# Left-over 64 channels of the projections as half-height matmul pairs, in units of two groups

## The chip, the cores and the metric

The kernel runs on one core of one Trainium2 chip. The metric is the device time of one execution in microseconds (us). A core has TensorE (PE in the profile; its weight loads are PEld), VectorE (DVE), ScalarE (ACT), GpSimd (POOL) and SyncE (SP, here only an issuer of DMAs), 16 DMA engines, the on-chip SBUF of 128 partitions and PSUM of 8 banks with 512 fp32 per partition.

## The reference

x has R = 128 rows, C = 192 columns and E = 192 channels. It is group-normalised, then goes through an attention with 12 heads of D = 16 channels in which two columns attend to each other, summed over all rows (row weights `sw` come from a softmax of their own). All in fp32.

```python
Q = (x @ Wq).reshape(B, R, C, H, D) * scaling * sw
K = (x @ Wk).reshape(B, R, C, H, D)
V = (x @ Wv).reshape(B, R, C, H, D)
QK = jnp.einsum('brihd,brjhd->bhij', Q, K)
...
attn = jax.nn.softmax(QK, axis=-1)
out = jnp.einsum('bhij,brjhd->brihd', attn, V)
...
x = x + _L0_conv_ref(_gn(x), ...)
```

## The kernel before

**Precision.** Each fp32 operand of a matmul is split into an fp16 high part and an fp16 low part, and a product is the sum of high x high, high x low and low x high.

**Prologue.** x is loaded, its statistics are taken on DVE (`statistics`, L600), and it is transposed chunk by chunk (a chunk is CI = 8 columns) by PE (`x_transposes`, L872), normalised on DVE and ACT, and split in high and low (ACT L492, DVE L694, POOL L442). SyncE stores the transposed chunks in pairs to a DRAM scratch `xt_dram` with seven transfers per pair (L333 to L339). In between PE computes the scores of the row weights (L927, L933). These are transposed back in three parts by `weights_back` (L962 to L964, the matmuls are at L949), and ACT copies each part to SW (L516, semaphore `s_sw`).

**Layout of the transposed x.** 192 channels are 128 + 64. A loaded chunk in XT[b] has three regions of 8 x 128 columns: the highs of the 128 channels, their lows, and a third region for the other 64 channels, whose upper and lower 64 partitions are, before, the highs and the lows of the same column. Eight columns stand as four even ones and four odd ones. The weights of the 64 channels stand twice in WP, in partitions 0 to 63 and 64 to 127.

**Projections.** There are two head halves, h = 0 and h = 1 (h0 and h1 below). `project(h, t, steps)` (L970) makes Q and K of six heads and V of all twelve for h0 (384 outputs per column, CW[0]), and Q and K of the other six heads for h1 (192, CW[1]). A group is SI[h] = 2 or 4 columns and fills two PSUM banks; four groups have buffers (`projected`, L243). A column takes five matmuls with the transposed x stationary and the weights moving:

```python
mm(po, xh0, WP[:, 0, 0, wc], start=True, stop=False)
mm(po, xh0, WP[:, 1, 0, wc], start=False, stop=False)
mm(po, xl0, WP[:, 0, 0, wc], start=False, stop=False)
mm(po, x1, WP[:, 0, 1, wc], start=False, stop=False)
ins = mm(po, x1, WP[:, 1, 1, wc], start=False, stop=True)
```

h0 has 96 groups, h1 48, unrolled by 8 in a hardware loop. For each group ACT copies the highs of V (L532, h0 only) and of K (L535); DVE multiplies Q by the row weights (L767), and subtracts for the lows of V (L773, h0 only) and K (L776, which frees the PSUM buffer, `s_kvl`); ACT copies the highs of Q (L521) and POOL subtracts for its lows (L451). PE waits ahead of group n for `s_kvl` of group n - 4 (L977), at a new chunk for its load (L976), and in the first turn of h0 for parts of the row weights (L981 to L984), whose banks it reuses; in the first turn of h1 for the last reads of the attention before it.

**SyncE in h0.** Chunks are loaded into two buffers (`load_xt`, L343). V goes to DRAM from two buffers, two transfers per chunk up to column 127 (L355), four with rows of 192 bytes from column 128 on (L359, `store_v`); ACT waits for the store of two chunks before (L531). In h1 there are four load buffers; the third and fourth lie where the attention of h0 had its last output tiles, so their first loads wait for output stores (L404).

**Attention.** Per head 16 x 5 matmuls (L1053 to L1057) and four fp32 transposes (L1038 to L1041) with softmax on DVE and ACT; then attention times V (L1024), the residual on DVE (L839) and stores issued by ACT (L569, L572).

## Time and profile before

| | us |
|---|---|
| median of 3 runs | 647.25 (646.57 to 648.66) |
| the profiled execution | 645.96 |
| its span in the trace | 644.2 |
| PE busy | 518.9 (81%), 4984 matmuls |
| DVE busy | 435.5 (68%) |
| ACT busy | 251.3 (39%) |
| POOL busy | 225.7 (35%) |
| HBM traffic | 95.60 MB read, 56.62 MB written |

The shares are averages over stages with different limits, so they are read by stage. "Busy" of PE is modelled from pipelined matmuls: one matmul's duration is longer than the distance to the next one's start, and what a matmul costs in a stream is that distance. The granted clock is a fraction of the higher of TensorE's two levels. A wait is shown as idle time with what ended it.

### The profile page before, as it was taken

The page shows a single profiled execution, that of the slowest core. Times are in us where ns is not written, and L with a number is a line of the kernel's source. Part 1 is how long each engine was busy: PE and PEld are TensorE (multiplying, and loading weights), DVE is VectorE, ACT ScalarE, POOL GpSimd, SP SyncE. Part 2 cuts the span into 40 slices and gives each one's busy share as a digit, 9 for nine tenths or more (in the row PEclk, how much of TensorE's full clock was granted, in tenths as well). Part 3 has the DMA queues.
Part 4 walks back from the last instruction along what each step waited for, and adds up shares of the span by engine and source line. Part 5 has one row for each costly group of instructions (what it writes and reads, how often), then busy time and mean ns, then how long its engine had stood idle before and what let it go on. Part 6 is the DMA issues. An engine that isn't in the chain of part 4 may idle for free.

```text
span 644.2 us, 14355 instructions
## 1 busy us (share of the span) xinstructions
PE 518.9 (81%) x4984; PEld 426.1 (66%) x4984; DVE 435.5 (68%) x981; ACT 251.3 (39%) x555; POOL 225.7 (35%) x231
## 2 busy tenths in 40 slices
PE   0040298998539999999998999969499997999884
PEld 0030177998416666666665998849499997998773
DVE  3899847799915666666665566936277774566954
ACT  0030236688306555555554111323255552112242
POOL 1010024688303333333333000638255663000674
PEclk9996557899559999999998999979799998999988
DMA  8993004798965888888998999999877766899998
GB/s 279 404 424 142 0 1 141 197 244 243 249 207 157 236 249 240 242 246 237 237 243 150 276 288 295 309 338 272 261 235 243 242 196 147 263 268 304 285 269 231
DMA packets 207258, 152.82 MB, mean 237 GB/s; under 512 B 170032, under 2 KB 190064, under 8 KB 206448
## 3 DMA queue, kind: packets, MB, share of 16 engines
q1 hardware_dynamic: 155296, 132.14, 70.5%
q10 hardware_dynamic: 51920, 20.11, 12.5%
q8 instruction: 28, 0.46, 0.3%
q14 instruction: 14, 0.11, 0.0%
HBM read 95.60 MB, written 56.62 MB: 236 GB/s over the span
## 4 chain that ended last, share of the span: by engine, by line
PE 64%; DVE 12%; SPq 7%; DMA 5%; ACTq 4%; issue 3%; POOL 3%; ACT 1%; POOLq 0%; DVEq 0%
PE PS L993 7%; PE PS L994 7%; PE PS L995 7%; PE PS L996 7%; PE PS L997 7%; DVE EXTRA L600 6%; PE PS L1024 6%; PE PS L872 3%; PE PS L1053 3%; DVE BIG L839 3%; PE PS L1054 3%; PE PS L1055 3%; PE PS L1056 3%; PE PS L1057 3%; PE PS L911 2%
## 5 line engine op out<-in xcount | busy, mean ns | idle before, releaser
L451 POOL TENSOR_TENSOR BIG<-EXTRA,BIG 128x192 f32 (+1 forms) x144 | 106.5, 740 | 165.8 <-ACT BIG L521 165.6
L767 DVE TENSOR_TENSOR EXTRA<-PS,SW 128x192 f32<-128x192 f32 (+1 forms) x144 | 73.2, 508 | 96.0 <-ACT BIG L535 95.7
L993 PE MATMUL PS<-WP,EXTRA 128*128 128x384 f16 (+1 forms) x384 | 111.0, 289 | 21.4 <-DMA EXTRA<-xt_scratch 21.4
L994 PE MATMUL PS<-WP,EXTRA 128*128 128x384 f16 (+1 forms) x384 | 111.1, 289 | 0.0
L995 PE MATMUL PS<-WP,EXTRA 128*128 128x384 f16 (+1 forms) x384 | 111.0, 289 | 0.0
L996 PE MATMUL PS<-WP,EXTRA 128*128 128x384 f16 (+1 forms) x384 | 110.8, 289 | 0.0
L997 PE MATMUL PS<-WP,EXTRA 128*128 128x384 f16 (+1 forms) x384 | 110.8, 288 | 0.0
L1024 PE MATMUL PS<-BIG,EXTRA 128*128 128x256 f16 x768 | 88.9, 279 | 10.2 <-ACT EXTRA L578 10.0
L459 POOL TENSOR_TENSOR BIG<-BIG,EXTRA 64x512 f32<-64x512 f32 x36 | 45.1, 1265 | 135.0 <-DVE BIG L839 108.9
L1024 PEld LDWEIGHTS PS<-BIG,EXTRA 128*128 128x128 f16 x768 | 75.8, 100 | 22.5 <-issue 10.2
L442 POOL TENSOR_TENSOR BIG<-EXTRA,BIG 128x1024 f16<-128x1024 f32 x24 | 53.4, 2227 | 71.2 <-ACT BIG L492 70.9
L535 ACT CAST BIG<-PS 128x192 f32 (+3 forms) x144 | 55.1, 383 | 43.8 <-PE PS L997 43.8
L532 ACT CAST EXTRA<-PS 128x384 f16<-128x384 f32 x96 | 46.0, 479 | 62.0 <-PE PS L997 50.5
L521 ACT CAST BIG<-EXTRA 128x192 f32 (+3 forms) x144 | 60.5, 420 | 2.0 <-DVE EXTRA L767 2.0
L839 DVE SCALAR_TENSOR_TENSOR BIG<-PS,small,BIG 128x512 f32<-128x512 f32 x72 | 49.0, 737 | 17.6 <-PE PS L1024 17.4
L993 PEld LDWEIGHTS PS<-WP,EXTRA 128*128 128x128 f16 x384 | 37.9, 99 | 34.3 <-issue 13.1
L776 DVE TENSOR_TENSOR BIG<-PS,BIG 128x192 f32 (+3 forms) x144 | 59.9, 416 | 0.0
L600 DVE BATCH_NORM_STATS2 EXTRA<-BIG 128x6 f32<-128x192 f32 x192 | 50.3, 335 | 13.4 <-DMA BIG<-in_x 13.3
L578 ACT ACTIVATE EXTRA<-PS,small 64x512 f32<-64x512 f32 x48 | 30.6, 681 | 60.9 <-PE PS L1024 27.2
L1053 PE MATMUL PS<-BIG 128*128 128x192 f16 x192 | 48.4, 252 | 5.9 <-POOL BIG L451 5.9
L773 DVE TENSOR_TENSOR EXTRA<-PS,EXTRA 128x384 f16<-128x384 f32 x96 | 52.6, 548 | 0.0
L872 PE MATMUL PS<-ident,BIG 128*128 128x128 f32 x288 | 45.0, 321 | 5.9 <-DVE EXTRA L637 4.2
(155 smaller groups left out, 931.2 us busy)
## 6 DMA issues: line engine op xcount, KB each, us to landing
EXTRA<-xt_scratch SPq DMA_DIRECT2D x48, 512.0 KB, 3.6
BIG<-in_x SPq DMA_DIRECT2D x6, 3072.0 KB, 21.6
EXTRA<-xt_scratch SPq DMA_DIRECT2D x48, 256.0 KB, 3.8
v_scratch<-EXTRA SPq DMA_DIRECT2D x32, 384.0 KB, 4.2
BIG<-v_scratch SPq DMA_DIRECT2D x16, 768.0 KB, 6.9
BIG<-in_x SPq DMA_DIRECT2D x12, 768.0 KB, 9.3
out_x<-BIG ACTq DMA_DIRECT2D x12, 768.0 KB, 6.8
xt_scratch<-BIG SPq DMA_DIRECT2D x12, 512.0 KB, 3.3
```

The source lines that it names most:

```text
L451: pool.tensor_tensor(QA[:, :, bass.ds(SI[h] * n + low, SI[h])], TQ[h][g % 4], QA[:, :, bass.ds(SI[h] * n, SI[h])], ALU.subtract).then_inc( ...
L600: ins = v.bn_stats(ST[:, g, c, :], xv[:, :, g * GC:(g + 1) * GC])
L767: v.tensor_tensor(TQ[h][g % 4].rearrange("p (m d) i -> p m d i", d=D), ps[:, :, 0:EH].rearrange("p i (m d) -> p m d i", d=D), swv.unsqueez ...
L839: v.scalar_tensor_tensor(o, PS[0:rows, attended_bank(m), :].rearrange("p (r e) -> p r e", r=RI), mxb[0:rows, WV:WV + 1], o, ALU.mult, ALU. ...
L872: ins = nc.tensor.transpose(PS[:, 3 * (c % 2) + k, q * P:(q + 1) * P], X[:, at:at + P], ident[:, :])
L993: mm(po, xh0, WP[:, 0, 0, wc], start=True, stop=False)
L994: mm(po, xh0, WP[:, 1, 0, wc], start=False, stop=False)
L995: mm(po, xl0, WP[:, 0, 0, wc], start=False, stop=False)
L996: mm(po, x1, WP[:, 0, 1, wc], start=False, stop=False)
L997: ins = mm(po, x1, WP[:, 1, 1, wc], start=False, stop=True)
L1024: ins = mm(po[:, :, a, :], stationary, moving, start=j == 0, stop=j == len(terms) - 1)
L1053: mm(p0, QA[:, m, 0:P], kh, start=first, stop=False)
```

## The change

1. `project` works on units of two groups (`for u in range(SPT[h] // 2)`): first all waits of both groups, then two parts, each for both groups. `full_rows` has the three matmuls per column on the 128 channels. `half_rows` has the 64 left-over channels: for two neighbouring columns three steps (high x high, high x low, low x high), in each of which one matmul uses partitions 0 to 63 for the even column and one partitions 64 to 127 for the odd one. The low x low product is gone. In every other unit the half part comes first.
2. The third region of XT therefore has the even column's highs and lows in partitions 0 to 63 and the odd column's in 64 to 127; the stores to DRAM go from seven to five per pair of chunks.
3. The two columns of a step lie in different PSUM banks. For h0 they did already; for h1 `projected` now lets neighbouring columns alternate between the two banks. The reads of ACT and DVE follow that: the product with the row weights is two instructions per group in h1, the copy and the subtraction of K have one more dimension.

```diff
--- before.py
+++ after.py
@@ -153,7 +153,7 @@
 
         s_x = [sem(f"x_loaded{c}") for c in range(NXC)]
         s_params = sem("params_loaded")
-        STORES = 16 * 7
+        STORES = 16 * 5
         V_STORED = 32 * 8 + 64 * 4
         s_wld = sem("weights_loaded")
         N_WEIGHTS = 5 * 3
@@ -244,7 +244,7 @@
 
             b = 2 * ((g + 3) % 4)
             ps = PS[:, b:b + 2, :]
-            return ps if h == 0 else ps.rearrange("p a (b n) -> p (a b) n", b=2)
+            return ps if h == 0 else ps.rearrange("p a (b n) -> p b a n", b=2)
 
 
 
@@ -326,17 +326,15 @@
                 sp.wait_ge(s_ld, c + 2)
                 stored = s_sp[min(c, 1)]
                 full = xt_dram[c // 2, :, 0:4 * CI * R].rearrange("p (c a n) -> p c a n", a=2, n=512)
-                rest = xt_dram[c // 2, :, 4 * CI * R:6 * CI * R].rearrange("p (c a n) -> p c a n", a=2, n=512)
+                rest = xt_dram[c // 2, :, 4 * CI * R:6 * CI * R].rearrange("p (c n) -> p c n", n=512)
                 src = BIG[:, c * CI * E:(c + 2) * CI * E].bitcast(fp16)
                 src = src.rearrange("p (c t n) -> p c t n", t=3, n=512)
                 even, mixed, odd = (src[:, :, t, :] for t in range(3))
                 sp.dma_start(full[:, :, 0, :], even).then_inc(stored, 16)
                 sp.dma_start(full[0:E1, :, 1, :], mixed[E1:P]).then_inc(stored, 16)
                 sp.dma_start(full[E1:P, :, 1, :], odd[0:E1]).then_inc(stored, 16)
-                for s in range(2):
-                    to = rest[s * E1:(s + 1) * E1]
-                    sp.dma_start(to[:, :, 0, :], mixed[0:E1, s::2, :]).then_inc(stored, 16)
-                    sp.dma_start(to[:, :, 1, :], odd[E1:P, s::2, :]).then_inc(stored, 16)
+                sp.dma_start(rest[0:E1], mixed[0:E1]).then_inc(stored, 16)
+                sp.dma_start(rest[E1:P], odd[E1:P]).then_inc(stored, 16)
             sp.wait_ge(s_sc, NCH // 2)
             sp.wait_ge(s_sp[0], STORES)
 
@@ -532,8 +530,13 @@
                             nc.scalar.copy(VS[b][:, at:at + SI[h], :, 0, :],
                                            ps[:, :, 2 * EH:2 * EH + E].rearrange("p i (h e) -> p i h e", h=2)
                                            ).then_inc(s_kvh[h], 1)
-                        nc.scalar.copy(KA[:, :, bass.ds(SI[h] * n, SI[h])],
-                                       ps[:, :, EH:2 * EH].rearrange("p i m -> p m i")).then_inc(s_kvh[h], 1)
+                        if h == 0:
+                            nc.scalar.copy(KA[:, :, bass.ds(SI[h] * n, SI[h])],
+                                           ps[:, :, EH:2 * EH].rearrange("p i m -> p m i")).then_inc(s_kvh[h], 1)
+                        else:
+                            nc.scalar.copy(KA[:, :, bass.ds(SI[h] * n, SI[h])].rearrange("p m (b a) -> p m b a", a=2),
+                                           ps[:, :, :, EH:2 * EH].rearrange("p b a m -> p m b a")
+                                           ).then_inc(s_kvh[h], 1)
                         if g or not isinstance(t, int):
                             q_high(n - 1, g - 1)
 
@@ -764,18 +767,25 @@
                         when(dve, s_ql[h], n - 3)
                         swv = SW[:, bass.ds(si * n * H, si * H)].rearrange("p (i m) -> p m i", m=H)
                         swv = swv[:, h * HALF:(h + 1) * HALF, :]
-                        v.tensor_tensor(TQ[h][g % 4].rearrange("p (m d) i -> p m d i", d=D),
-                                        ps[:, :, 0:EH].rearrange("p i (m d) -> p m d i", d=D),
-                                        swv.unsqueeze(2).to_broadcast([P, HALF, D, si]),
-                                        ALU.mult).then_inc(s_tq[h], 1)
+                        tq = TQ[h][g % 4].rearrange("p (m d) i -> p m d i", d=D)
+                        for i in range(0, si, 2):
+                            pq = ps[:, :, 0:EH] if h == 0 else ps[:, i // 2, :, 0:EH]
+                            ins = v.tensor_tensor(tq[:, :, :, i:i + 2], pq.rearrange("p i (m d) -> p m d i", d=D),
+                                                  swv[:, :, i:i + 2].unsqueeze(2).to_broadcast([P, HALF, D, 2]),
+                                                  ALU.mult)
+                        ins.then_inc(s_tq[h], 1)
                         if h == 0:
                             vs = VS[b][:, at:at + si, :, :, :]
                             v.tensor_tensor(vs[:, :, :, 1, :],
                                             ps[:, :, 2 * EH:2 * EH + E].rearrange("p i (h e) -> p i h e", h=2),
                                             vs[:, :, :, 0, :], ALU.subtract)
-                        v.tensor_tensor(KA[:, :, bass.ds(si * n + C, si)],
-                                        ps[:, :, EH:2 * EH].rearrange("p i m -> p m i"),
-                                        KA[:, :, bass.ds(si * n, si)], ALU.subtract).then_inc(s_kvl[h], 1)
+                        kl, kh = (KA[:, :, bass.ds(si * n + o, si)] for o in (C, 0))
+                        if h == 0:
+                            pk = ps[:, :, EH:2 * EH].rearrange("p i m -> p m i")
+                        else:
+                            pk = ps[:, :, :, EH:2 * EH].rearrange("p b a m -> p m b a")
+                            kl, kh = (q.rearrange("p m (b a) -> p m b a", a=2) for q in (kl, kh))
+                        v.tensor_tensor(kl, pk, kh, ALU.subtract).then_inc(s_kvl[h], 1)
 
                 if h:
                     dve.wait_ge(s_lo[0], NB)
@@ -967,35 +977,52 @@
 
             pe.wait_ge(s_wl, len(W_PARTS))
 
-            def project(h, t, steps):
+            def project(h, t):
                 wc = slice(h * CW[0], h * CW[0] + CW[h])
-                for g in steps:
-                    n = SPT[h] * t + g
-                    b, at = divmod(g * SI[h], CI)
-                    if at == 0:
-                        pe.wait_ge(s_xt[h][b], 32 * (t + 1))
-                    when(pe, s_kvl[h], n - 3)
-                    if h and isinstance(t, int) and g < 4:
-                        pe.wait_ge(s_ad[0], 2 * NB - 6 + 2 * g)
-                        pe.wait_ge(s_ol[0], NB - 3 + g)
-                    if h == 0 and isinstance(t, int) and g in range(1, PARTS + 1):
-                        if g < PARTS:
-                            weights_back(g)
-                        pe.wait_ge(s_sw, g)
-                    ps = projected(h, g)
+
+                def full_rows(ps, b, at, opens):
                     for i in range(SI[h]):
-                        il = at + i
-                        po = ps[:, i, 0:CW[h]]
-                        slot = (il % 2) * (CI // 2) + il // 2
+                        po = ps[:, i, 0:CW[h]] if h == 0 else ps[:, i // 2, i % 2, 0:CW[h]]
+                        slot = ((at + i) % 2) * (CI // 2) + (at + i) // 2
                         xh0 = XT[b][:, slot * R:(slot + 1) * R]
                         xl0 = XT[b][:, (CI + slot) * R:(CI + slot + 1) * R]
-                        x1 = XT[b][:, (2 * CI + slot) * R:(2 * CI + slot + 1) * R]
-                        mm(po, xh0, WP[:, 0, 0, wc], start=True, stop=False)
-                        mm(po, xh0, WP[:, 1, 0, wc], start=False, stop=False)
-                        mm(po, xl0, WP[:, 0, 0, wc], start=False, stop=False)
-                        mm(po, x1, WP[:, 0, 1, wc], start=False, stop=False)
-                        ins = mm(po, x1, WP[:, 1, 1, wc], start=False, stop=True)
-                    ins.then_inc(s_pj[h], 1)
+                        for j, (xs0, w) in enumerate(((xh0, 0), (xh0, 1), (xl0, 0))):
+                            ins = mm(po, xs0, WP[:, w, 0, wc], start=opens and i < 2 and j == 0,
+                                     stop=not opens and j == 2, skip_group_check=True)
+                    return ins
+
+                def half_rows(ps, b, at, opens):
+                    for even in range(0, SI[h], 2):
+                        for j, (s, w) in enumerate(((0, 0), (0, 1), (1, 0))):
+                            for i, rows in ((0, slice(0, E1)), (1, slice(E1, P))):
+                                po = ps[:, i, 0:CW[h]] if h == 0 else ps[:, even // 2, i, 0:CW[h]]
+                                o = (2 * CI + s * (CI // 2) + (at + even) // 2) * R
+                                ins = mm(po, XT[b][rows, o:o + R], WP[rows, w, 1, wc],
+                                         start=opens and even == 0 and j == 0, stop=not opens and j == 2,
+                                         skip_group_check=True)
+                    return ins
+
+                for u in range(SPT[h] // 2):
+                    for g in (2 * u, 2 * u + 1):
+                        n = SPT[h] * t + g
+                        b, at = divmod(g * SI[h], CI)
+                        if at == 0:
+                            pe.wait_ge(s_xt[h][b], 32 * (t + 1))
+                        when(pe, s_kvl[h], n - 3)
+                        if h and isinstance(t, int) and g < 4:
+                            pe.wait_ge(s_ad[0], 2 * NB - 6 + 2 * g)
+                            pe.wait_ge(s_ol[0], NB - 3 + g)
+                        if h == 0 and isinstance(t, int) and g in range(1, PARTS + 1):
+                            if g < PARTS:
+                                weights_back(g)
+                            pe.wait_ge(s_sw, g)
+                    parts = (full_rows, half_rows) if u % 2 == 0 else (half_rows, full_rows)
+                    for j, part in enumerate(parts):
+                        for g in (2 * u, 2 * u + 1):
+                            b, at = divmod(g * SI[h], CI)
+                            ins = part(projected(h, g), b, at, j == 0)
+                            if j:
+                                ins.then_inc(s_pj[h], 1)
 
             def attended(h, m):
                 (n, hp), t = BLOCK[m // 2], m % 2
@@ -1026,9 +1053,9 @@
 
             for h in range(2):
 
-                project(h, 0, range(SPT[h]))
+                project(h, 0)
                 with pe.Fori(1, TURNS[h]) as t:
-                    project(h, t, range(SPT[h]))
+                    project(h, t)
 
                 def transposes(k):
                     lg = LG[k % 2]
```

Lines of the changed kernel are numbered anew: L990 is the matmul of `full_rows`, L1000 that of `half_rows`, L959 the transposes of `weights_back`, L773 and L788 DVE's product and subtraction of K.

PE in the body of h0's loop. Before, one group (two columns) of eight:

```order
L237 REGISTER_ALU
L993 MATMUL PS<-WP,EXTRA 128x384
L994 MATMUL PS<-WP,EXTRA 128x384
L995 MATMUL PS<-WP,EXTRA 128x384
L996 MATMUL PS<-WP,EXTRA 128x384
L997 MATMUL PS<-WP,EXTRA 128x384
L993 MATMUL PS<-WP,EXTRA 128x384
L994 MATMUL PS<-WP,EXTRA 128x384
L995 MATMUL PS<-WP,EXTRA 128x384
L996 MATMUL PS<-WP,EXTRA 128x384
L997 MATMUL PS<-WP,EXTRA 128x384
```

Now, all eight groups, in four units:

```order
L990 MATMUL PS<-WP,EXTRA 128x384 x12
L1000 MATMUL PS<-WP,EXTRA 128x384 x12
L237 REGISTER_ALU
L1000 MATMUL PS<-WP,EXTRA 128x384 x12
L990 MATMUL PS<-WP,EXTRA 128x384 x12
L237 REGISTER_ALU x2
L990 MATMUL PS<-WP,EXTRA 128x384 x12
L1000 MATMUL PS<-WP,EXTRA 128x384 x12
L237 REGISTER_ALU x2
L1000 MATMUL PS<-WP,EXTRA 128x384 x12
L990 MATMUL PS<-WP,EXTRA 128x384 x12
```

Ten matmuls per group have become twelve, six of them half-height (L1000), and these stand in runs of 24 but for the seams of the loop.

PE at the start of h0, with what it waits for. Before:

```order
L949 MATMUL PS<-ident,EXTRA 128x128 [waits row_weights_normalised]
L949 MATMUL PS<-ident,EXTRA 128x128 x5
L993 MATMUL PS<-WP,EXTRA 128x384 [waits row_weights_ready]
```

Now:

```order
L990 MATMUL PS<-WP,EXTRA 128x384 [waits row_weights_ready]
L990 MATMUL PS<-WP,EXTRA 128x384 x11
L1000 MATMUL PS<-WP,EXTRA 128x384 x12
L959 MATMUL PS<-ident,EXTRA 128x128 [waits row_weights_normalised]
L959 MATMUL PS<-ident,EXTRA 128x128 x5
L1000 MATMUL PS<-WP,EXTRA 128x384 [waits row_weights_ready]
```

The wait behind the last transposes is now for all three parts of the row weights, the one just issued included, where before it was for two, and the third was waited for a group later.

SyncE's list for one pair of chunks in the prologue. Before:

```order
L333 DMA xt_scratch<-BIG 128x4x512
L334 DMA xt_scratch<-BIG 64x4x512
L335 DMA xt_scratch<-BIG 64x4x512
L338 DMA xt_scratch<-BIG 64x2x512
L339 DMA xt_scratch<-BIG 64x2x512
L338 DMA xt_scratch<-BIG 64x2x512
L339 DMA xt_scratch<-BIG 64x2x512
```

Now:

```order
L333 DMA xt_scratch<-BIG 128x4x512
L334 DMA xt_scratch<-BIG 64x4x512
L335 DMA xt_scratch<-BIG 64x4x512
L336 DMA xt_scratch<-BIG 64x4x512
L337 DMA xt_scratch<-BIG 64x4x512
```

Four transfers of 64 x 2 runs have become two of 64 x 4.

## Rows read from the trace of the kernel before

**Rows 1.** Busy time by stage: us, then engines, granted clock, DMA share, GB/s.

```profile
188.00:349.50 161.50, 160.00 (x972) 96.32 (x971) 103.05 (x287) 92.74 (x290) 57.32 (x95) 0.98 0.87 221
...
463.00:538.00 75.00, 74.23 (x880) 73.83 (x880) 55.12 (x86) 38.59 (x87) 43.12 (x43) 0.98 0.66 217
```

**Rows 2.** Timeline of PE in h0: start us, us, instruction.

```profile
250.34 0.33 PE L993 MATMUL PS<-WP,EXTRA 128*128 128x384 f16 x1
...
251.96 0.33 PE L993 MATMUL PS<-WP,EXTRA 128*128 128x384 f16 x1
```

**Rows 3.** Timeline of PE and its weight loads (PEld) in h1.

```profile
489.94 0.25 PE L993 MATMUL PS<-WP,EXTRA 128*128 128x192 f16 x1
...
490.03 0.10 PEld L995 LDWEIGHTS PS<-WP,EXTRA 128*128 128x128 f16 x1
...
491.60 0.25 PE L993 MATMUL PS<-WP,EXTRA 128*128 128x192 f16 x1
```

**Rows 4.** Timeline of DVE catching up at the start of h0.

```profile
197.80 0.35 DVE L767 TENSOR_TENSOR EXTRA<-PS,SW 128x192 f32<-128x192 f32 x1
...
198.80 0.35 DVE L767 TENSOR_TENSOR EXTRA<-PS,SW 128x192 f32<-128x192 f32 x1
```

**Rows 5.** Timeline of PE, first projection matmul.

```profile
187.91 0.48 PE L993 MATMUL PS<-WP,EXTRA 128*128 128x384 f16 x1 [12.59 <-DMA EXTRA<-xt_scratch]
```

**Rows 6.** Waits at h1's loads: who for whom, us, times, longest.

```profile
PE PS L993 <- DMA EXTRA<-xt_scratch: 8.8, 1, 8.8
```

**Rows 7.** Timeline of PE and PEld, one round of attention transposes.

```profile
365.26 0.27 PE L1038 MATMUL PS<-ident,EXTRA 128*128 128x128 f32 x1
...
365.46 0.14 PEld L1039 LDWEIGHTS PS<-ident,EXTRA 64*128 64x128 f32 x1
...
365.46 0.27 PE L1039 MATMUL PS<-ident,EXTRA 64*128 64x64 f32 x1
...
366.12 0.10 PEld L1053 LDWEIGHTS PS<-BIG 128*128 128x128 f16 x1
366.13 0.26 PE L1053 MATMUL PS<-BIG 128*128 128x192 f16 x1
```

**Rows 8.** Timeline at the third part of the row weights.

```profile
194.43 0.82 PE L949 MATMUL PS<-ident,EXTRA 128*128 128x128 f32 x6
...
195.29 0.80 ACT L516 COPY SW<-PS 128x768 f32<-128x768 f32 x1 [1.91 <-PE PS L949]
```

**Rows 9.** Timeline of SyncE's queue, ACT and DVE in the last third of h0.

```profile
324.17 3.83 SPq L359 DMA_DIRECT2D v_scratch<-EXTRA  x4
...
331.67 0.48 ACT L532 CAST EXTRA<-PS 128x384 f16<-128x384 f32 x1 [2.17 <-DMA v_scratch<-EXTRA]
...
333.26 0.36 DVE L776 TENSOR_TENSOR BIG<-PS,BIG 128x192 f32 x1
```

**Rows 10.** Groups of h1 by line and shape: busy us, mean ns, idle before.

```profile
L451 POOL TENSOR_TENSOR BIG<-EXTRA,BIG 128x384 f32 x45 | 45.2, 1005 | 34.8 <-ACT BIG L521 34.8
...
L767 DVE TENSOR_TENSOR EXTRA<-PS,SW 128x384 f32<-128x384 f32 x44 | 35.8, 814 | 22.5 <-ACT BIG L535 22.5
L776 DVE TENSOR_TENSOR BIG<-PS,BIG 128x384 f32 x40 | 22.0, 550 | 0.0
```

**Rows 11.** Timeline of SyncE's queue, the last stores and the first load.

```profile
176.89 0.55 SPq L333 DMA_DIRECT2D xt_scratch<-BIG  x1
...
182.18 0.61 SPq L339 DMA_DIRECT2D xt_scratch<-BIG  x1
182.89 0.54 SPq L347 DMA_DIRECT2D EXTRA<-xt_scratch  x1
```

**Rows 12.** Busy time by single us in the store stage, columns as Rows 1.

```profile
171.00:172.00 1.00, 0.42 (x2) 0.45 (x3) 1.00 (x3) 0.84 (x1) 0.00 (x0) 0.50 0.59 144
...
179.00:180.00 1.00, 0.00 (x0) 0.00 (x0) 0.97 (x2) 0.00 (x0) 0.00 (x0) 0.50 1.00 291
180.00:181.00 1.00, 0.00 (x0) 0.00 (x0) 0.14 (x1) 0.00 (x0) 0.00 (x0) 0.50 0.95 207
```

## The prediction

> **What bounds the kernel now.** I read the busy times by stage first [rows 1]. In the two projection stages, from 188.0 to 349.5 us (first head half, in short h0) and from 463 to 538 us (second half, h1), the matmul row of TensorE (PE) is busy 160.0 of 161.5 us and 74.2 of 75.0; every other engine sits well below. Then the timeline of PE: in h0 the same line returns after one group of ten matmuls in 1.62 us [rows 2], so a matmul of 384 columns costs 0.162 us; in h1 it returns after twenty in 1.66 us [rows 3], so one of 192 columns costs 0.083 us. [...] So whatever shortens PE's list there shortens the run, until the next thing binds. I looked for that in three places: VectorE (DVE), which can serve h0 groups at a start-to-start of 1.00 us against PE's 1.62 [rows 4] (ScalarE, ACT, is busy 92.7 us of the stage [rows 1]); the stores of V in the last third of h0; and the head of the stage, where PE stands still 12.59 us until the first transposed x arrives [rows 5].
>
> **Fewer slots.** Call one full matmul time a slot. Before, a column takes 5 slots. Now it takes 3 full-height ones, and two columns share 3 steps in each of which one half-height matmul runs in rows 0 to 63 and another in rows 64 to 127. If the two of a step run at once, a column takes 4.5. h0: 96 groups of two columns, 10 slots become 9, 96 x 0.162 = **15.6 us less**. h1: 48 groups of four, 20 become 18, 0.166 each. The first four groups of h1 run before PE's wait of 8.8 us for a load [rows 6], so their gain is swallowed: 44 x 0.166 = **7.3 less**.
>
> **Does a pair really take one slot?** No row of before shows matmuls of two row groups alternating, so this is bounded. Best: nothing extra. Worst: one after the other, two slots a step; there are 3 x 96 steps in either half, 288 x (0.162 + 0.083) = 70.6 us. [...]
>
> **Switches of array shape.** Every unit of two groups goes once between full and half height (the reversed order in every other unit keeps the seams without one): 48 in h0, 24 in h1, 2 of them before the swallowed wait, so 70. The nearest rows are the four transposes of the attention stage, alternately 128 and 64 rows high [rows 7]. From the first one's start to the next full matmul's is 366.13 - 365.26 = 0.87 us with four changes. The same transposes with no change take 0.82 / 6 = 0.137 each [rows 8], and if the two small ones take half, 0.41 for all. The rest, 0.46, is 0.115 per change. They are fp32, whose weight load takes 0.14 against 0.10 [rows 7], so I take 0.08: 70 x 0.08 = **5.6 more**; ends 0 and 8.
>
> **Start of h0.** Two groups are now opened together, so all their waits stand ahead of both. The transposes of the third part of the row weights are issued ahead of group 2, and the wait for ACT's copy of them (group 3's) is right behind. Before, group 2's 1.6 us covered it. The copy starts 0.04 us after the transposes and takes 0.80 [rows 8], so with the signals PE waits about 1.0: **1.0 more** (0.8 to 1.2).
>
> **Rhythm of pairs.** Four buffers in PSUM are now two double ones: a unit waits for both groups of the unit before last. In h0 the second group of a unit is ready at T, the first 0.49 us earlier; ACT and DVE drain a group in 333.26 + 0.36 - 331.67 = 1.95 us when they start fresh [rows 9] and the second follows 1.0 behind [rows 4], about T + 2.5; it is due at T + 18 x 0.162 = T + 2.9. No wait, 0.4 us of slack. In h1 DVE's product took 0.81 [rows 10] and is now two of the form that takes 0.36 in h0 [rows 4]: 0.72, no loss. The subtraction (0.55 [rows 10]) now reads banks in another order; if it took 0.81 too, 0.72 + 0.81 = 1.53 against 1.50 per group would just bind, 1 to 2 us; I take 0. At the end of h1 the last two groups finish 0.5 us apart instead of 1.66, while GpSimd (POOL) takes 1.0 for each [rows 10]: attention waits **0.5 more**.
>
> **V stores.** From column 128 on V leaves in rows of 192 bytes. The four issues of a chunk take 3.83 us from 324.17 and ACT waits for their landing until 331.67 [rows 9], 7.5 us; PE does not feel it today because it is up to three groups ahead. ACT needs the V buffer two chunks later. With period P per chunk of 8 columns, the buffer is back at (last drained group) + 0.2 + 7.0 to 7.5, and PE stalls when that is later than the end of the next-but-one chunk's first unit: 1.5 P = 2.3 + 0.2 + 7.25, P = 6.5 us. That is today's period. So the 6 chunks for which this holds gain nothing of the net 0.4 each (6.5 less 36 slots of 0.162, two switches and the pairs' fixed part): **2.4 more** (0 to 4, as the transfers vary).
>
> **Stores of the transposed x.** Per chunk pair 7 transfers become 5; bytes and run lengths stay. At the end of the prologue SyncE issues back to back, 6.0 us per pair [rows 11], and the first projection waits behind that. Is it the issuing or the transfer? The DMA engines are 0.95 to 1.00 busy in the middle of a pair but 0.59 around its last two issues [rows 12], where 128 KB go out per 0.65 us. Larger issues close this hole: at full share 6.0 becomes about 5.6, times 10 pairs, 4 us; up to 6 if more of the waste goes. Against it: a transfer that touches only 64 partitions moved 207 GB/s in its microsecond, where it overlaps the 128-partition one 291 [rows 12], and the new order has two lower-half transfers of 256 KB in succession; that can cost 0.4 per pair, 4 in all. I take **1.5 less** (6 less to 4 more). ACT, DVE and POOL carry the same work in the prologue.
>
> **Sum.** -15.6 - 7.3 + 1.4 + 5.6 + 1.0 + 0.5 + 2.4 - 1.5 = -13.5. The profiled execution took 645.96 us (span 644.2 and 1.8 around it), so 632.5; the median of the runs is 1.3 above it, 647.25, so **633.8 us**. What follows (attention, output stores, the second half) only moves earlier; it depends on the stage's end, not on a clock of its own, except for the swallowed 8.8 us wait, which is for output stores that also move.
>
> **Rivals.**
> Weight loads come out of cover, or the halves queue (slower). If a half-height load could not run under its own rows' matmul, every step would show a load of 0.10 us [rows 3]: 576 x 0.10 = 57.6 us, 691 us; if the halves ran one after the other, 70.6 - 1.4, 703 us. It turns slower than before as soon as a step costs over 1.21 slots (14.9 us of 70.6, what the sum leaves plus the 1.4). For it: nothing in the trace shows two at once. Against: full-height loads do run under the matmul before them (the load at 490.03 lies inside the matmul from 489.94 that lasts 0.25 [rows 3]). [...] Chance 0.13.
> Consumers bind: switches at 0.115 (2.4 more), V stores at their upper end (1.6), the subtraction slow (2), and a pair 1.02 slots (1.5): 641 us. For it: the slack of 0.4 us is thin. Chance 0.17.
> The prologue opens: 6 less instead of 1.5, switches half as dear: 626.5 us. For it the hole in the DMA share; against it the half-partition rate. Chance 0.12.
> The change gives back what it takes, at a step of 1.18 to 1.24 slots: 645.3 to 649.2 us. Chance 0.04.
> The forecast itself: 0.54, own range 629 to 639.
>
> **Numbers.** This kernel's runs differ by 0.3% (2 us), about what can be told from no change. The likeliest time is 633.8. The range reaches below the prologue case and through the consumers' case to 645 above; the slow rival stays out. Faster by over 0.3%: 0.54 + 0.17 + 0.12 = 0.83; within: 0.04; slower: 0.13.
>
> **What would show it.** Half-height matmuls start in twos, the next two 0.162 us on in h0 and 0.083 in h1; a gap of about 0.24 us at a change of height in h0; the h0 stage near 154 us, h1 from the end of its 8.8 us wait near 71; PE's first projection near 186; chunks of 5.9 to 6.1 us up to column 128 and 6.5 behind. Wrong would be: starts of half-height matmuls a full slot apart (they queue), PE waits on VectorE in every unit (the rhythm binds), or a store pair of over 6.4 us (half partitions bind).

## The result and the profile after

The changed kernel took 629.89 us (median of 6 runs, 625.05 to 632.36), the kernel before 646.59 in the same rounds; the ratio is 0.9728, 95% interval 0.9697 to 0.9759: faster, inside the range, 3.9 us below the forecast of 633.8. The profiled execution took 631.34 us, its span is 629.5, 14.7 us less than before.

The two projection stages of the changed kernel by busy time, columns as in [rows 1]; each starts when the load that PE waited for has landed and ends at the first matmul of the attention:

```profile
182.97:337.54 154.57, 150.20 (x1164) 82.40 (x1165) 100.44 (x288) 92.94 (x290) 58.58 (x96) 0.99 0.91 231
451.27:525.15 73.88, 70.54 (x1056) 66.40 (x1057) 45.78 (x132) 40.25 (x89) 45.14 (x45) 0.96 0.71 227
```

Against the same cuts of before (187.91 to 350.52, 463.32 to 540.92 us) the whole 14.7 us divide so:

| stretch | before | after | difference | in the forecast's sum |
|---|---|---|---|---|
| prologue, to the first load's landing | 187.91 | 182.97 | -4.9 | -1.5 |
| h0 | 162.61 | 154.57 | -8.0 | -7.7 |
| attention of h0, to h1's late load | 112.80 | 113.73 | +0.9 | 0 |
| h1 from there | 77.60 | 73.88 | -3.7 | -4.3 |
| the rest | 103.3 | 104.4 | +1.1 | 0 |

(The forecast's terms by stage: h0 is -15.6 with 0.7 for the pairs, 3.8 for 48 switches, 1.0 and 2.4; h1 is -7.3 with 0.7, 1.8 and 0.5.) The two stretches without a term differ by no more than profiles of kernels that leave them alone do among each other: in the experiments below, other than V in longer rows, the third stretch took 111.7 to 115.3 us and the last 100.6 to 104.8.

The timeline of PE in the middle of h0, where before [rows 2] stood; a line now merges neighbours of one kind. The first two lines are from a window of 0.1 us, so the second is what had started by 250.5; the other two are from the whole stretch:

```profile
250.15 0.33 PE L990 MATMUL PS<-WP,EXTRA 128*128 128x384 f16 x1
250.41 0.34 PE L1000 MATMUL PS<-WP,EXTRA 64*128 64x384 f16 x2
```

```profile
250.41 2.12 PE L1000 MATMUL PS<-WP,EXTRA 64*128 64x384 f16 x24
252.46 0.82 PE L990 MATMUL PS<-WP,EXTRA 128*128 128x384 f16 x4
```

Two half-height matmuls start together. Twenty-four of them occupy PE from 250.41 to 252.46, 2.05 us for twelve steps of which each would be 0.162 alone, 1.94. And the change of height is visible from both sides: 0.26 us from the last full-height start to the first half-height one instead of 0.162, and 0.11 left over at the other end.

The start of h0, where [rows 5] and [rows 8] stood:

```profile
182.97 1.51 PE L959 MATMUL PS<-ident,EXTRA 128*128 128x128 f32 x6 [7.34 <-DMA EXTRA<-xt_scratch]
184.28 3.60 PE L990 MATMUL PS<-WP,EXTRA 128*128 128x384 f16 x12
187.81 1.15 PE L1000 MATMUL PS<-WP,EXTRA 64*128 64x384 f16 x12
188.89 0.88 PE L959 MATMUL PS<-ident,EXTRA 128*128 128x128 f32 x6
190.75 1.15 PE L1000 MATMUL PS<-WP,EXTRA 64*128 64x384 f16 x12 [0.98 <-ACT SW L514]
191.83 4.07 PE L990 MATMUL PS<-WP,EXTRA 128*128 128x384 f16 x24
```

The load lands 4.9 us earlier, and PE then waits 0.98 us for ACT's copy of the third part. SyncE's queue at the end of the prologue, where [rows 11] stood (the first issue of the last pair of chunks, its last two, and the first load):

```profile
171.43 0.43 SPq L333 DMA_DIRECT2D xt_scratch<-BIG  x1
174.14 1.08 SPq L336 DMA_DIRECT2D xt_scratch<-BIG  x1
175.26 1.09 SPq L337 DMA_DIRECT2D xt_scratch<-BIG  x1
176.45 1.06 SPq L345 DMA_DIRECT2D EXTRA<-xt_scratch  x1
```

Five issues take 5.0 us (171.43 to 176.45) where seven took 6.0, and the first load goes out at 176.45 instead of 182.89. Over the seven pairs before the last one a pair takes 5.80 us on average, where it took 6.44. By single microseconds, columns as in [rows 12]:

```profile
171.00:172.00 1.00, 0.10 (x1) 0.13 (x2) 1.00 (x3) 0.60 (x1) 0.00 (x0) 0.50 0.80 206
172.00:173.00 1.00, 1.00 (x6) 1.00 (x6) 0.93 (x3) 0.24 (x1) 0.00 (x0) 0.50 1.00 232
173.00:174.00 1.00, 0.41 (x2) 0.01 (x1) 0.97 (x3) 0.00 (x0) 0.00 (x0) 0.50 1.00 333
174.00:175.00 1.00, 0.91 (x5) 0.91 (x5) 0.96 (x3) 0.00 (x0) 0.00 (x0) 0.50 1.04 320
```

In the microsecond at the seam to the last pair, the DMA engines are at 0.80 where [rows 12] had 0.59, and behind it at 1.00 to 1.04. From 140 to 179 us the lowest microsecond of this profile is 0.80, that of the profile before 0.53.

The last third of h0: the first matmuls of two chunks, with PE's wait for DVE, and then ACT's wait for V's store.

```profile
315.77 2.12 PE L990 MATMUL PS<-WP,EXTRA 128*128 128x384 f16 x12 [0.28 <-DVE BIG L788]
322.19 2.12 PE L990 MATMUL PS<-WP,EXTRA 128*128 128x384 f16 x12 [0.18 <-DVE BIG L788]
```

```profile
319.19 0.48 ACT L530 CAST EXTRA<-PS 128x384 f16<-128x384 f32 x1 [2.67 <-DMA v_scratch<-EXTRA]
```

From 315.77 to 322.19 a chunk takes 6.42 us, where 6.06 is the pace of the chunks up to the middle of the stage. The wait is short because it is the last link: V's store makes ACT 2.67 us late, ACT makes DVE late, and PE finds the first unit's buffers 0.2 to 0.3 us too late.

### The profile page after: what moved, and what is told of

It reads as the page before. It is cut to its first block, busy times and chain, and to the rows that moved or that the text cites. A ratio compares the mean times of both kernels' runs of the same rounds, so it can differ in the third digit from the quotient of the medians.

```text
span 629.5 us, 15205 instructions
## 1 busy us (share of the span) xinstructions
PE 505.7 (80%) x5368; PEld 403.9 (64%) x5368; DVE 422.6 (67%) x1029; ACT 252.1 (40%) x555; POOL 225.3 (36%) x231
## 4 chain that ended last, share of the span: by engine, by line
PE 58%; DVE 18%; DMA 7%; SPq 5%; issue 4%; ACTq 3%; ACT 2%; POOL 2%; POOLq 0%; DVEq 0%
PE PS L990 19%; PE PS L1000 10%; PE PS L1051 7%; DVE EXTRA L603 7%; DVE BIG L849 5%; PE PS L882 3%; PE PS L1080 3%; PE PS L1081 3%; PE PS L1084 3%; PE PS L1082 3%; PE PS L1083 3%; PE PS L921 2%; DMA v_scratch<-EXTRA 2%; DVE EXTRA L709 2%; ACTq L575 2%
## 5 line engine op out<-in xcount | busy, mean ns | idle before, releaser
L990 PE MATMUL PS<-WP,EXTRA 128*128 128x384 f16 (+1 forms) x1152 | 152.0, 291 | 9.5 <-DMA EXTRA<-xt_scratch 8.7
L990 PEld LDWEIGHTS PS<-WP,EXTRA 128*128 128x128 f16 x1152 | 103.0, 99 | 55.7 <-issue 11.0
L773 DVE TENSOR_TENSOR EXTRA<-PS,SW 128x192 f32<-128x192 f32 x192 | 63.8, 353 | 93.1 <-ACT BIG L534 56.1
L1051 PE MATMUL PS<-BIG,EXTRA 128*128 128x256 f16 x768 | 90.2, 281 | 11.3 <-ACT EXTRA L581 11.2
L1000 PE MATMUL PS<-WP,EXTRA 64*128 64x384 f16 (+1 forms) x1152 | 78.0, 285 | 1.1 <-ACT SW L514 1.0
L1000 PEld LDWEIGHTS PS<-WP,EXTRA 64*128 64x128 f16 x1152 | 50.0, 95 | 26.7 <-issue 10.0
L519 ACT CAST BIG<-EXTRA 128x192 f32 (+3 forms) x144 | 61.9, 430 | 3.0 <-DVE EXTRA L773 2.1
L788 DVE TENSOR_TENSOR BIG<-PS,BIG 128x192 f32 (+3 forms) x144 | 60.5, 420 | 0.0
L1080 PE MATMUL PS<-BIG 128*128 128x192 f16 x192 | 48.4, 252 | 6.0 <-POOL BIG L449 6.0
L1081 PE MATMUL PS<-BIG 128*128 128x192 f16 x192 | 48.3, 252 | 0.0
L1082 PE MATMUL PS<-BIG 128*128 128x192 f16 x192 | 48.2, 251 | 0.0
L1084 PE MATMUL PS<-BIG 128*128 128x192 f16 x192 | 48.2, 251 | 0.0
```

What stands on the lines that cost most here:

```text
L773: ins = v.tensor_tensor(tq[:, :, :, i:i + 2], pq.rearrange("p i (m d) -> p m d i", d=D), swv[:, :, i:i + 2].unsqueeze(2).to_broadcast([P, ...
L990: ins = mm(po, xs0, WP[:, w, 0, wc], start=opens and i < 2 and j == 0, stop=not opens and j == 2, skip_group_check=True)
L1000: ins = mm(po, XT[b][rows, o:o + R], WP[rows, w, 1, wc], start=opens and even == 0 and j == 0, stop=not opens and j == 2, skip_group_check ...
L1051: ins = mm(po[:, :, a, :], stationary, moving, start=j == 0, stop=j == len(terms) - 1)
L1080: mm(p0, QA[:, m, 0:P], kh, start=first, stop=False)
L1081: mm(p0, QA[:, m, 0:P], kl, start=False, stop=False)
```

## The experiments

All edits are against the changed kernel, each run beside the kernel before and compared through the ratio to it. They come in three groups, each on one chip: first the order within the six, the same order in every unit, the seven stores and which half follows which; then both matmuls in the same half, longer blocks, units of one group and the later wait; last V in longer rows and the changed kernel beside the later wait again. The edits are shown shortened where three dots stand.

### The order within the six half-height matmuls

```diff
-for j, (s, w) in enumerate(((0, 0), (0, 1), (1, 0))):
-    for i, rows in ((0, slice(0, E1)), (1, slice(E1, P))):
+for i, rows in ((0, slice(0, E1)), (1, slice(E1, P))):
+    for j, (s, w) in enumerate(((0, 0), (0, 1), (1, 0))):
```

> The changed kernel, but of the six half-height matmuls of a column pair the three in partitions 0 to 63 come first and then the three in 64 to 127, instead of alternating. Slot theory (two neighbours of different halves run at once, same half queues): within a block of three of one half nothing can overlap except at the one seam, so a pair of columns takes about 5 slots where it took 3; 96 x 2 x 0.162 + 96 x 2 x 0.083 = 47 us more than the changed kernel, about 677 us. Rival (the half-height matmuls are cheaper for another reason, such as fewer active rows): the order within the six would not matter, within 2 us of the changed kernel.

Measured 632.1 us, ratio 0.9769 (0.9741 to 0.9798). The slot theory as I had put it fell: the order cost nothing that shows, and h0 takes 154.6 us as in the changed kernel. Its timeline, first what had started by 251.6, then whole:

```profile
251.53 0.34 PE L1000 MATMUL PS<-WP,EXTRA 64*128 64x384 f16 x2
```

```profile
251.53 2.13 PE L1000 MATMUL PS<-WP,EXTRA 64*128 64x384 f16 x24
253.60 0.66 PE L990 MATMUL PS<-WP,EXTRA 128*128 128x384 f16 x3
```

They still start in twos, 24 in 2.07 us, although the second of the list uses the same rows as the first. Either TensorE fetches a matmul of the other half from further down its queue, or a half-height matmul costs half wherever it lies. The next run tells these apart.

### Both matmuls of a step in the same half

```diff
-for i, rows in ((0, slice(0, E1)), (1, slice(E1, P))):
+for i, rows in ((0, slice(0, E1)), (1, slice(0, E1))):
```

> The changed kernel with both matmuls of every step in partitions 0 to 63 (the odd column's left-over channels are replaced by the even column's; the rest is as changed). In the run with blocks of three the half-height matmuls still started in twos. Theory (two halves overlap, and TensorE looks past at least three waiting matmuls of the same half): without a matmul of the other half nothing overlaps, a step takes two slots, up to 70 us more than the changed kernel, about 700 us. Rival (a half-height matmul simply costs half, whichever rows it uses): within 2 us of the changed kernel, 630 us.

This kernel leaves out the odd columns' left-over channels, so only its time is of use. Measured 694.5 us, ratio 1.0742 (1.0676 to 1.0808), 64.6 us above the changed kernel:

```profile
252.52 4.07 PE L1000 MATMUL PS<-WP,EXTRA 64*128 64x384 f16 x24
256.52 0.66 PE L990 MATMUL PS<-WP,EXTRA 128*128 128x384 f16 x3
```

24 matmuls now take 4.00 us: 24 x 0.1625 = 3.90 and one change of height. A half-height matmul costs a whole slot; the gain is the overlap of the two halves and nothing else. h0 is 45.3 us longer than in the changed kernel, for 288 steps at 0.1625 = 46.8; the waits of its last third, 1.6 us, are absent here.

### Longer blocks of one half

```diff
+blocks = ((0, slice(0, E1)), (1, slice(E1, P))) if part is half_rows else ((),)
+for block in blocks:
     for g in (2 * u, 2 * u + 1):
...
```

> The changed kernel with all matmuls of partitions 0 to 63 of a unit first (6 in a row in h0, 12 in h1), then all of 64 to 127. Blocks of three cost nothing. Theory (TensorE looks ahead over a window of some instructions, loads included): the longer the blocks the less overlaps; if the window holds 6 matmuls h0 stays and h1 gains at most 6 steps per unit of 12, 0.5 us x 22 = 11 us more; if it holds fewer, up to 24 x 6 x 0.162 for h0 more. Rival (halves run on queues of their own of any length): within 2 us of the changed kernel.

Measured 646.6 us, ratio 0.9998 (0.9964 to 1.0033): this order alone gives the whole gain back. A stretch of h0 and one of h1:

```profile
220.35 2.46 PE L1000 MATMUL PS<-WP,EXTRA 64*128 64x384 f16 x24
222.75 4.07 PE L990 MATMUL PS<-WP,EXTRA 128*128 128x384 f16 x24
```

```profile
475.44 3.20 PE L1000 MATMUL PS<-WP,EXTRA 64*128 64x192 f16 x48
478.57 1.66 PE L990 MATMUL PS<-WP,EXTRA 128*128 128x192 f16 x18
```

The same stretch of h1 in the changed kernel:

```profile
468.34 2.15 PE L1000 MATMUL PS<-WP,EXTRA 64*128 64x192 f16 x48
470.43 1.74 PE L990 MATMUL PS<-WP,EXTRA 128*128 128x192 f16 x19
```

Start to start of the runs: with blocks of 6 in h0 2.40 us instead of 2.05; with blocks of 12 in h1 3.13 instead of 2.09. So TensorE looks ahead past the two waiting matmuls of a block of three at no cost, but not freely past 5 or 11. Where it stops is in the same trace. What had started by 220.68 and by 220.70 in h0, and by 476.10 and 476.13 in h1:

```profile
220.35 0.50 PE L1000 MATMUL PS<-WP,EXTRA 64*128 64x384 f16 x2
220.35 0.68 PE L1000 MATMUL PS<-WP,EXTRA 64*128 64x384 f16 x4
```

```profile
475.44 0.83 PE L1000 MATMUL PS<-WP,EXTRA 64*128 64x192 f16 x8
475.44 0.93 PE L1000 MATMUL PS<-WP,EXTRA 64*128 64x192 f16 x10
```

The first matmuls stand alone, a slot apart. The first one of the other half starts with the third of six, and with the ninth of twelve: both times three of the first block still wait. From that the runs can be added up: the other half starts 2 slots late in h0, so 24 take 14 slots (2.28 us, and 0.11 for the change of height; measured 2.40). In h1 a block of twelve starts 8 slots behind the one before it, so four take 3 x 8 + 12 = 36 slots (2.97 us, and 0.11; measured 3.13). The look-ahead in this program is three waiting matmuls of the other half. Whether it is counted in matmuls or in instructions with their weight loads, the runs don't tell.

### Every unit in the same order

```diff
-parts = (full_rows, half_rows) if u % 2 == 0 else (half_rows, full_rows)
+parts = (full_rows, half_rows)
```

> The changed kernel with the full-height part first in every unit, so two changes of height per unit instead of one: 48 + 24 = 72 more of them. The trace of the changed kernel shows 0.10 us each (last full-height start 250.15 to first half-height start 250.41, of which 0.162 is the slot). Theory: 72 x 0.10 = 7 us slower than the changed kernel, a bit less for the last third of h0 where V stores bind. Rival (a change of height costs nothing by itself, the 0.10 is hidden by the rhythm of the pairs or by the waits): within 2 us of the changed kernel.

Measured 635.45 us, ratio 0.9775 (0.9701 to 0.9849). The four runs spread from 626.6 to 637.8 us and the interval is too wide for 5 us, so the steps inside the trace decide (it is of the longest of the four; the next run shows the same 3.14 us):

```profile
220.07 2.12 PE L990 MATMUL PS<-WP,EXTRA 128*128 128x384 f16 x12
222.13 1.15 PE L1000 MATMUL PS<-WP,EXTRA 64*128 64x384 f16 x12
223.21 2.12 PE L990 MATMUL PS<-WP,EXTRA 128*128 128x384 f16 x12
```

A unit takes 223.21 - 220.07 = 3.14 us with two changes of height. Over fifteen chunks of mid-stage h0 (two units each) a chunk takes 6.276 us here, 6.063 in the changed kernel and 6.500 before, so two more changes are 0.213: **0.107 us per change**. h0 is 4.5 us longer (48 x 0.107 = 5.1, less in the last third, where V's store binds), h1 2.5 longer. The rival, that the change costs nothing by itself, is out. The same figures price the pairs: a slot is 6.500 / 40 = 0.1625 us, and 36 slots and two changes are 5.85 + 0.21 = 6.06, all that a chunk takes. Nothing is left for the second matmul of a step.

### Units of one group

```diff
-for u in range(SPT[h] // 2):
-    for g in (2 * u, 2 * u + 1):
+for u in range(SPT[h]):
+    for g in (u,):
...
-        for g in (2 * u, 2 * u + 1):
+        for g in (u,):
```

> The changed kernel with units of one group (waits of one group only, order still reversed in every other unit). 72 more changes of height at 0.10 us are 7.2 us more; the last third of h0 and the start of h0 (no wait of 1.0 us for the third part of the row weights) give back 1 to 2. About 5 to 6 us slower than the changed kernel. Rival (the pairing of waits costs as much as the changes it saves, because PE stalls on buffers freed in pairs): within 1.5 us.

Measured 632.5 us, ratio 0.9801 (0.9752 to 0.9850), 2.6 above the changed kernel's 629.9, between the two expectations; the interval overlaps the changed kernel's. The full-height parts of every second group:

```profile
220.38 2.12 PE L990 MATMUL PS<-WP,EXTRA 128*128 128x384 f16 x12
223.52 2.12 PE L990 MATMUL PS<-WP,EXTRA 128*128 128x384 f16 x12
```

Two groups take 3.14 us as in the run before, so a change costs the same and the waits of pairs cost nothing in mid-stage. h0 is 2.5 us longer, not 5.0: this kernel has no wait for the third part of the row weights, and no waits of PE on DVE in the last third, because 6.28 us per chunk is nearly V's pace (6.4 to 6.5). Its first load also landed at 180.54, 2.4 earlier, with the same stores: the prologue scatters by as much, and that hides part of the difference in the total.

### Seven stores again

```diff
-STORES = 16 * 5
+STORES = 16 * 7
...
-sp.dma_start(rest[0:E1], mixed[0:E1]).then_inc(stored, 16)
-sp.dma_start(rest[E1:P], odd[E1:P]).then_inc(stored, 16)
+for k in (slice(0, 2), slice(2, 4)):
+    sp.dma_start(rest[0:E1, k], mixed[0:E1, k]).then_inc(stored, 16)
+    sp.dma_start(rest[E1:P, k], odd[E1:P, k]).then_inc(stored, 16)
```

> The changed kernel with the left-over channels stored in four transfers of 128 KB per pair of chunks instead of two of 256 KB; everything else as changed. Theory A (the hole that small issues leave in the DMA share was the price): the first projection starts near 187.5 us again instead of 183.0, 4 to 5 us slower than the changed kernel. Theory B (the 4.9 us at the start came from something else, such as which halves follow each other): start within 1 us of 183 and time within 1 us of the changed kernel.

Measured 636.6 us, ratio 0.9845 (0.9819 to 0.9870), 6.7 above the changed kernel. SyncE's queue, and the DMA share just behind the two small issues that end at 170.6 us:

```profile
182.90 0.61 SPq L338 DMA_DIRECT2D xt_scratch<-BIG  x1
183.61 0.54 SPq L346 DMA_DIRECT2D EXTRA<-xt_scratch  x1
```

```profile
171.00:172.00 1.00, 0.00 (x0) 0.00 (x0) 0.97 (x3) 0.00 (x0) 0.00 (x0) 0.50 0.73 170
172.00:173.00 1.00, 0.43 (x2) 0.46 (x3) 1.00 (x3) 0.84 (x1) 0.00 (x0) 0.50 0.48 164
```

The first load is issued at 183.61 (176.45 in the changed kernel, 182.89 before) and lands at 188.79 (182.97, 187.91). A pair takes 6.41 us on average, as before the change. So the prologue's gain comes from fewer and larger issues for the same bytes: theory A. (Number and size changed together; nothing here parts them.) Of the 6.7 us some 0.9 is not the prologue: after the later landing PE stays at the lower clock level (granted 0.50) for 6.1 us instead of 4.3, and h0 is 0.9 longer for it.

### Which partition half follows which

```diff
-sp.dma_start(rest[0:E1], mixed[0:E1]).then_inc(stored, 16)
 sp.dma_start(rest[E1:P], odd[E1:P]).then_inc(stored, 16)
+sp.dma_start(rest[0:E1], mixed[0:E1]).then_inc(stored, 16)
```

> The changed kernel with the last two stores of a pair of chunks swapped, so that the four 64-partition transfers go upper, lower, upper, lower instead of upper, lower, lower, upper. If consecutive transfers of the same partition half bind (my reason to keep the prologue's gain small), the first projection starts 2 to 4 us earlier than 183. If not, within 1 us, and the time within 1 us.

Measured 627.9 us, ratio 0.9689 (0.9632 to 0.9746). The first load lands at 182.41, 0.6 earlier. Over all profiles with five stores it lands at 180.5 to 184.4 in the given order (eight profiles, mean 182.7) and at 181.6 to 182.4 in the alternating one (three, mean 181.9), so the 2 to 4 us that my reason asked for are not there; whether one microsecond is, stays open.

### The wait for the third part, later

This kernel has the alternating stores of the run before as well.

```diff
+    if g < PARTS:
-    pe.wait_ge(s_sw, g)
+        pe.wait_ge(s_sw, g)
...
+if h == 0 and isinstance(t, int) and g == PARTS and j == 0:
+    pe.wait_ge(s_sw, g)
 ins = part(projected(h, g), b, at, j == 0)
```

> The changed kernel with the alternating order of the half-partition stores and with the wait for the third part of the row weights moved behind group 2's half-height part. The wait of 0.98 us before the first half-height matmul of the second unit goes to under 0.3 us, if it is that wait; 0.5 to 1 us less than the alternating order alone (627.9), which runs can hardly tell but the trace can.

Measured 628.5 us, ratio 0.9739 (0.9690 to 0.9787): not below the 627.9 us (0.9689) of the alternating stores alone, and the intervals overlap. The same kernel ran again beside the changed one:

> The changed kernel as it is, on the same chip and in the same rounds as the next, to compare the two: 0.973 of the kernel before, 629 to 631 us.

> The changed kernel with the alternating store order and the late wait. If the two bring 0.7 and 1 us together, 1 to 2 us below the changed kernel in these rounds, ratio about 0.971; if the order of the stores does nothing, 0.5 to 1 us below.

Measured 630.4 us and 0.9726 (0.9678 to 0.9775) for the changed kernel, 626.9 us and 0.9688 (0.9643 to 0.9734) with both edits. The start of h0 with them:

```profile
188.01 0.88 PE L959 MATMUL PS<-ident,EXTRA 128*128 128x128 f32 x6
189.78 0.66 PE L1000 MATMUL PS<-WP,EXTRA 64*128 64x384 f16 x6 [0.30 <-ACT SW L514]
190.38 2.12 PE L990 MATMUL PS<-WP,EXTRA 128*128 128x384 f16 x12
192.66 2.11 PE L990 MATMUL PS<-WP,EXTRA 128*128 128x384 f16 x12 [0.16 <-DVE BIG L788]
```

The wait is 0.30 us instead of 0.98, but it doesn't all arrive as gain: the next unit now waits for DVE. From the transposes to the thirteenth full-height matmul behind them it is 192.66 - 188.01 = 4.65 us, in the changed kernel 191.83 + 12 x 0.1625 - 188.89 = 4.89. So 0.24 us of gain is shown. h0 as a whole, with 154.6 and 155.3 us, is no shorter than the changed kernel's 154.6 and 154.7. The medians with both edits are lower than the changed kernel's (628.5 and 626.9 against 629.9 and 630.4), but the first ratio is not, and the intervals overlap: a gain beyond the 0.24 is not shown.

### V in longer rows

```diff
-v1_dram = nc.dram_tensor("v1_scratch", [2, 2, E1, R, EH], fp16, kind="Internal").ap()
+v1_dram = nc.dram_tensor("v1_scratch", [2, E1, R, 2 * EH], fp16, kind="Internal").ap()
...
-for k in range(2):
-    sp.dma_start(v1_dram[h, k, ...], VS[b][:, :, h, k, :]).then_inc(s_vs[b], 16)
+sp.dma_start(v1_dram[h, ...], VS[b][:, :, h, :, :] ...).then_inc(s_vs[b], 16)
...
+for s in range(2):
+    sp.dma_start(V1[k][s * E1:(s + 1) * E1],
+                 v1_dram[h, :, r0:r0 + RI, s * EH:(s + 1) * EH]).then_inc(s_vl[k], 16)
```

> The changed kernel with another layout of V's second scratch, so that a chunk from column 128 on leaves in two transfers with rows of 384 bytes instead of four with rows of 192; the price is that V's reload for the attention reads the second scratch in 192-byte pieces. Theory (the stores of V bind the last third of h0): the units of the last chunks go back to 3.03 us each (chunk period 6.07 instead of 6.4 to 6.5), the waits of PE on VectorE (0.7 us) and of ScalarE on V's store vanish, and attention of h0 starts 1 to 1.5 us earlier relative to the first projection (154.6 us now). The total is no measure here: 32 reloads of 2048 small pieces may cost far more later. Rival (the last third is slow for DVE or ScalarE's sake): the periods stay at 6.4 to 6.5.

Measured 636.9 us, ratio 0.9821 (0.9758 to 0.9883): its two attention stretches, where V is read back, take 116.9 and 108.8 us instead of 113.7 and 104.4. In the last third of h0:

```profile
311.20 2.12 PE L1000 MATMUL PS<-WP,EXTRA 64*128 64x384 f16 x24
317.26 2.12 PE L1000 MATMUL PS<-WP,EXTRA 64*128 64x384 f16 x24
```

The period is 6.06 us to the end (these are the half-height runs of two chunks), PE never waits for DVE, and h0 takes 152.95 us from landing to attention instead of 154.57. So V's stores cost the changed kernel 1.6 us.

## Why the prediction was right, and where its sizes were off

**What bounds** was right: PE's list bound both projection stages, and a shorter list shortened them.

**Fewer slots, and pairs at one slot** was right, and the most uncertain step. Steps stand 0.1625 us apart (twelve in 2.05 less one change of height), one slot to the resolution of the trace. The 1.4 us that the sum adds for the pairs as a fixed part of each second matmul were my estimate. No run shows them: at 0.1625 us a step costs one slot and nothing on top. The run with both in one half shows what the other end would have been: 694.5 us against the 703 of the rival. Nor does any step have the load of 0.10 us that the rival's other form put on each: they stand at the 0.1625 of a full-height matmul.

**Switches** were 0.107 us each, not 0.08: 70 of them 7.5 us instead of 5.6. I had derived 0.115 from the fp32 transposes [rows 7] and taken off for the cheaper fp16 load (0.10 us against 0.14). The 0.137 us per transpose in that working was a misreading: six lasted 0.82 us, but the next matmul started 0.66 after them, so one costs 0.11:

```profile
194.43 0.82 PE L949 MATMUL PS<-ident,EXTRA 128*128 128x128 f32 x6
195.09 0.33 PE L993 MATMUL PS<-WP,EXTRA 128*128 128x384 f16 x1
```

With 0.11 the same rows give 0.135 per change. The price that the runs show is 0.107 us.

**Start of h0** was right in what waits for what, and 0.4 us too small. The 0.98 us of the profile count from the modelled end of the transposes. The matmul starts 190.75 - 188.89 = 1.86 us after them where 0.66 is possible, so PE stands still 1.2 us, and going from half height to the full-height transposes adds one change of height: 1.3 to 1.4 in all. Counted over the whole first chunk, with the time at the lower clock level taken out, it is 1.36.

**Rhythm of pairs.** In mid-stage no wait, as forecast. DVE's product in h1 became two of 0.351 us, and the subtraction kept 0.548 us in its new order of banks; the feared 0.81 did not come:

```profile
L773 DVE TENSOR_TENSOR EXTRA<-PS,SW 128x192 f32<-128x192 f32 x88 | 27.2, 351 | 30.2 <-ACT BIG L537 27.7 <-POOL BIG L449 2.5
L788 DVE TENSOR_TENSOR BIG<-PS,BIG 128x384 f32 x40 | 21.9, 548 | 0.0
```

The 0.5 us for a queue on POOL at the end of h1 did not come: the wait of PE there is 3.34 us and was 3.37.

**The clock** has no term in the forecast. In both stages PE comes out of its wait for a load at the lower of its two levels (granted 0.50, against 1.00), with matmuls at twice the distance: in the profile before 0.32 us instead of 0.1625 at 384 columns, 0.16 instead of 0.083 at 192. Behind the late load of h1, after and before:

```profile
451.27:456.80 5.53, 5.53 (x45) 4.94 (x47) 0.00 (x0) 0.39 (x2) 0.00 (x0) 0.50 0.97 362
463.32:466.30 2.98, 2.98 (x19) 2.82 (x20) 0.00 (x0) 0.00 (x0) 0.00 (x0) 0.50 1.00 370
```

The first four groups behind that wait take 8.84 us instead of 6.15 at the higher level, and took 8.06 instead of 6.60: 1.2 us more are lost, and that is why h1 gained 3.7 and not 5. It is chance: in the experiments with the same 6.15 us per four groups afterwards, these first four take 7.4 to 8.6 us. At the head of h0 it went the other way: 4.3 us at the lower level after landing instead of 5.4, so 0.5 us less lost.

**V stores** cost 1.6 us, not 2.4: the period is 6.4 to 6.5 us as forecast (6.5), but it bit only in the last four or so chunks, since PE's lead had to be used up first. (By its own numbers the net per chunk was 6.5 - 6.02 = 0.48, so 2.9 and not 2.4; the pairs' fixed part in it is the same estimate, which no run shows.)

**Stores of the transposed x** is the term that was mis-sized most: 4.9 us in the two profiles against my 1.5, and 5.8 between the mean landing of the two profiles with seven stores (188.3) and that of the eleven with five (182.5, singly 180.5 to 184.4). The term's range had held it (up to 6). The hole of 0.59 in the DMA share was the right sign: the sum of it, 0.4 us per pair, was close to the 0.6 that a pair gained. What failed was the counterweight: I let the 207 GB/s of a microsecond in which a 64-partition transfer ran [rows 12] stand for the rate of such transfers, and laid 0.4 us per pair against the gain. The profile after moves 320 GB/s in the microsecond from 174, in the midst of 64-partition transfers, and the 1.5 MB of the last pair are issued in 5.0 us; the run with alternating halves gained nothing like the 4 us. One microsecond is no rate.

**The sum**: -13.5 forecast, -14.7 in the profiles, -16.7 between medians. By terms, measured less forecast: prologue -3.4, pairs -1.4, V -0.8, POOL -0.5, switches +1.9, start of h0 +0.4, the clock +0.7 (h1 +1.2, h0 -0.5), stretches in which nothing was changed +2.0; -1.1 in all, which makes -14.6. The list of PE's work and waits adds up in each stage to 0.1 us. That the total came within 4 us of the forecast is in part luck: the terms miss by 6.1 us on one side and 5.0 on the other, and the last two of them, 2.7 us, scatter by as much between profiles of the same instructions.

## What to carry to other kernels

Left-over channels of 64 can be laid in both partition halves with different columns, and two half-height matmuls then cost one slot, if the halves alternate (24 in 2.05 us), or change every three (24 in 2.07; their outputs were in different PSUM banks throughout; the same bank was not tried). A change between full and half height cost 0.107 us, so group the half-height ones and reverse the order of every other group. What a matmul costs in a stream is the distance to the next start, also for a handful of transposes; its duration in the profile is longer (0.33 us against 0.1625 for one of 384 columns, 0.82 against 0.66 for six transposes). Whether a queue of DMAs is held up by issuing is worth looking for in single microseconds around its smallest issues: here the share fell to 0.53 before and 0.39 with seven stores again, and merging four transfers of 128 KB into two of 256 KB brought 0.6 us per pair of chunks. Five-store profiles had such microseconds too (0.59 to 0.85 at the lowest), so the share points to the run to make, and doesn't replace it.

## What the runs showed of the hardware that I had not expected

- TensorE does not keep the order of its list between row groups: with three matmuls of one half ahead of three of the other the halves still start in twos and cost nothing (24 in 2.07 us, against 2.05 when they alternate); with six ahead it is 2.40 us, and with twelve of half the width 3.13 against 2.09. The other half starts when three of the block ahead still wait.
- A half-height matmul without a partner costs what a full-height one does (24 in 4.00 us with one change of height, 0.1625 each).
- An issue on SyncE's queue of a 64-partition transfer took 0.59 us at least, whether it carried 128 or 256 KB; the shortest of 128 partitions and 512 KB took 0.37 to 0.55.
